# The second weighing of a block moved two places up in TensorE's order of a step

## The chip, the core and the metric

The kernel runs on one core of a Trainium2 chip. The metric is the device time of one execution in microseconds (us); of several executions the median is given. The engines are TensorE (PE; its weight loads are listed apart as PEld), VectorE (DVE), ScalarE (ACT), GpSimd (POOL) and SyncE (SP, which issues the DMAs). Each engine works through its own list of instructions in order; semaphores tie the lists together.

## What is computed

The input is x of 4 sequences of 512 tokens with 128 channels. A layer norm and an RWKV time mixing come first, then a layer norm and six layers of local attention and a gated feed-forward block, all in float32. Nearly all the time goes to the six layers; the part that this case touches is the attention:

```python
qkv = x @ Wqkv                      # 128 -> 3 * 1024, 16 heads of 64
q = l2norm(q) * qs; k = l2norm(k) * ksc
q = q * cos * scale + rotate_half(q) * sin * scale
k = k * cos * inv + rotate_half(k) * sin * inv
sim = einsum('bhwie,bhwje->bhwij', bq, bk2) * QK_SCALE   # windows of 32, each with the one before
attn = softmax(where(mask, -big, sim), -1)
out = einsum('bhwij,bhwje->bhwie', attn, bv2)
x = out @ Wo + x
```

After each attention comes `a * gelu(gate) @ W2 + b2` on a layer-normed, token-shifted x.

## The kernel before

**Blocks and steps.** An item is one sequence in one layer: 6 x 4 = 24 items. An item has 4 blocks of 128 tokens, so there are 96 blocks. The main loop (function `transformer`) runs over steps, one new block for each, software-pipelined: in step s TensorE projects block s, turns and scores q and k of block s-2, and finishes block s-3. `t = step % 4` is the place of the step in its item. The feed-forward work of an item is spread over the steps t = 3 (`centre`, `variance`), t = 0 (`widen_rstd`, `expand` 0 and 1) and t = 1 (`expand` 2, `contract`) that follow.

**What sets the order.** Every engine has a list written out by hand, one loop body for each engine. There is no scheduler. TensorE's step is, in this order: `project` V0, `project` Q0, `turn_qk(step - 2, 0)`, at t = 1 `expand` 2, at t = 3 `centre`, `project` Q1, at t = 0 `widen_rstd`, `weigh(step - 3, 1)`, `turn_o(step - 3, 0)`, `score(step - 2)`, `turn_o(step - 3, 1)`, `project` K0 and K1, `turn_qk(step - 1, 3)`, `merge_heads`, at t = 1 `contract`, `turn_probs` twice, the rest of the feed-forward, `project` V1, `turn_qk(step - 1, 2)`, `weigh(step - 2, 0)`, `turn_qk(step - 1, 1)`, at t = 0 `expand` 1.

**The calls by their lines.** `project` is three matmuls of 128x512 (L1202 to L1204). `turn_qk` is four transposes of a rotated and normed part of q or k (L1212); ACT copies the result to `q_t` or `k_t` (L1074). `score` is two mask matmuls (L1236) and 64 small matmuls q by k (L1246). `weigh` is 32 small matmuls of probabilities by v (L1284) into `wide`. Each small matmul stands in the trace as two weight loads and two matmuls, so `weigh` is 64 loads and 64 matmuls and `score` is 128 and 128. `turn_o` is four transposes of the weighed values (L1299), `merge_heads` the output projection (L1313), `widen_rstd` four transposes (L1341) that wait for the root of the norms, DVE's L922. `expand` is L1357 and L1358, `centre` L1324.

**The waits around `weigh(g, 1)`.** It waits only for `o_normed[0]` of its block: DVE must have read the first half of `wide` (L946, L949) before the second weighing overwrites it. Its own result goes to DVE's second L946 and L949. DVE's step is: nine small operations of the root (L914 to L922), `rotate` 0 (L879, L885), L946 and L949 for half 1, `rotate` 1, `maximum` (L928) twice, `shift` (L936) and sums of squares (L895), `rotate` 2 and 3, and at its end L946 and L949 for half 0 of the next block. ACT copies both halves of q (L1074) ahead of `square` 0 (L1064) and the first copy of o (L1095). `turn_o(g, 0)` waits for `o_normed[0]` and for the copy of the first half of q, whose bank it writes; `score` waits for the copies of all four parts of q and k, and for several reads of its two banks.

Of the kernel before, what the change touches and what calls it, by code (L numbers as in the profile page):

```python
# [82 lines left out]
def need(eng, sem, value, most=None):  # L83

    value = value if most is None else min(value, most)
    if value > 0:
        eng.wait_ge(sem, value)
# [531 lines left out]
def transformer(nc, bank, wide, weights, w_qkv, w_o, w_1, w_2, ident, center, mean_col, x_state, vecs, qk_rows,  # L619
# [12 lines left out]
    with ExitStack() as ctx:  # L632
# [59 lines left out]
        def live(g):  # L692
            return 0 <= g < BLOCKS
# [487 lines left out]
        def _(pe):  # L1181
# [24 lines left out]
            def turn_qk(g, c, before, value):  # L1206
                if not live(g):
                    return
                pe.wait_ge(normed[c], g + 1)
                need(pe, before, value)  # L1210
                for j in range(4):
                    mm = pe.transpose(bank[2 + c % 2][:, j * P:(j + 1) * P],  # L1212
                                      qk[:, g % 2, c, j * P:(j + 1) * P], ident[:])
                mm.then_inc(qk_turned[c], 1)
# [120 lines left out]
            def widen_rstd(m):  # L1335
                if not real(m):
                    return
                g = NBLK * (m + 1) + NBLK - 1
                pe.wait_ge(rooted, root_count(g))
                for j in range(NBLK):  # L1340
                    mm = pe.transpose(bank[4][:, j * P:(j + 1) * P],  # L1341
                                      rnorm[:, g % 2, NORMS + j:NORMS + j + 1].to_broadcast([P, P]), ident[:])
                mm.then_inc(rstd_wide, 1)
# [36 lines left out]
            for step in range(STEPS):  # L1380
                item, t = divmod(step, NBLK)
                project(step, V0)
                project(step, Q0)
                turn_qk(step - 2, 0, qk_taken[2], step - 1)
                if t == 1:
                    expand(item - 2, 2)
# [2 lines left out]
                project(step, Q1)  # L1389
                if t == 0:  # L1390
                    widen_rstd(item - 2)
                weigh(step - 3, 1)
                turn_o(step - 3, 0)
                score(step - 2, step)
                turn_o(step - 3, 1)
# [46 lines left out]
```

## Time and profile before

| | before |
|---|---|
| median of 3 runs | 1769.03 us (1767.48 to 1780.83) |
| the profiled execution: whole time | 1768.05 us |
| the profiled execution: span | 1766.3 us |
| mean granted TensorE clock | 0.97 of full |
| PE busy | 1612.7 us (91%) |
| DVE busy | 1445.9 us (82%) |
| ACT busy | 1106.9 us (63%) |
| POOL busy | 998.8 us (57%) |

The span is the time from the first to the last instruction of the profiled execution. Busy time is the time in which an engine has an instruction running. The chain is followed back from the last instruction, at each step to what released it; "issue" in it is time in which the engine waited for nothing that the profile shows.

### The profile page before, as it was taken

How to read it: one execution, taken by the hardware profiler on the slowest of the kernel's cores; microseconds unless marked ns; L12 is line 12 of the kernel's file. 1: busy time of each engine (PE TensorE's matmuls, PEld its weight loads, DVE VectorE, ACT ScalarE, POOL GpSimd, SP SyncE). 2: the span in 40 equal slices, each digit the busy share in tenths (PEclk: the TensorE clock that was granted, in tenths of full speed). 3: DMA queues.
4: the chain of work that ended last, by engine and by line, in shares of the span. 5: the costliest groups of instructions: out<-in, count | busy, mean ns of one | idle time of the engine just before them, and what ended most of it. 6: DMA issues, size and time to landing. Idle time of an engine off the chain costs nothing.

```text
span 1766.3 us, 75410 instructions
## 1 busy us (share of the span) xinstructions
PE 1612.7 (91%) x31917; PEld 1243.7 (70%) x32013; DVE 1445.9 (82%) x3189; ACT 1106.9 (63%) x1990; POOL 998.8 (57%) x956
## 2 busy tenths in 40 slices
PE   5369998999899999999999999999999999999985
PEld 2137776777777777777778777777777777777763
DVE  8769887888788888888888888888888888878861
ACT  5236666667566666666766766666766666766652
POOL 2246655665556566556576567476467476465530
PEclk8579999999999999999999999999999999999997
DMA  3011101111111111201111111111111111011010
GB/s 103 26 52 37 51 24 48 45 42 36 51 36 39 48 35 39 60 24 51 48 36 40 39 45 51 44 40 39 36 47 52 40 43 39 28 50 51 24 45 13
DMA packets 40597, 74.95 MB, mean 42 GB/s; under 512 B 8992, under 2 KB 22088, under 8 KB 40264
## 3 DMA queue, kind: packets, MB, share of 16 engines
q1 hardware_dynamic: 40264, 70.11, 13.6%
q8 instruction: 257, 4.21, 1.0%
q14 instruction: 76, 0.62, 0.1%
HBM read 20.08 MB, written 2.10 MB: 13 GB/s over the span
## 4 chain that ended last, share of the span: by engine, by line
PE 82%; issue 5%; DVE 4%; POOL 2%; ACT 1%; DVEq 0%; POOLq 0%; ACTq 0%
PE bank L1212 9%; PE bank L1313 9%; PE wide L1284 8%; PE bank L1246 8%; PE bank L1202 7%; PE bank L1204 7%; PE bank L1203 7%; PE bank L1299 6%; PE bank L1264 4%; PE bank L1357 4%; PE bank L1358 4%; PE bank L1368 4%; PE bank L1236 2%; PE bank L1324 1%; PE bank L1332 1%
## 5 line engine op out<-in xcount | busy, mean ns | idle before, releaser
L795 POOL TENSOR_TENSOR qk<-qk,qk_sin 128x512 f32<-128x512 f32 x384 | 492.2, 1282 | 215.4 <-DVE qk_sin L885 215.4
L803 POOL TENSOR_TENSOR qk<-qk,rnorm 128x512 f32<-128x512 f32 x384 | 401.8, 1047 | 352.9 <-DVE rnorm L922 352.9
L1064 ACT ACTIVATE squares<-bank 128x512 f32<-128x512 f32 x384 | 229.1, 597 | 159.1 <-DVE qk_sin L885 157.3
L1202 PE MATMUL bank<-w_hi,xs_hi 128*128 128x512 f32 x576 | 290.4, 504 | 12.9 <-ACT squares L1064 6.9
L895 DVE TENSOR_REDUCE norm<-squares 128x8 f32<-128x512 f32 x384 | 258.3, 678 | 31.1 <-ACT squares L1064 28.9
L879 DVE TENSOR_TENSOR qk<-bank,tables 128x512 f32<-128x512 f32 x384 | 261.5, 681 | 6.4 <-PE bank L1204 5.4
L885 DVE TENSOR_TENSOR qk_sin<-bank,tables 128x512 f32<-128x512 f32 x384 | 261.0, 680 | 0.0
L1212 PE MATMUL bank<-ident,qk 128*128 128x128 f32 x1536 | 237.2, 278 | 2.6 <-POOL qk L803 1.8
L1204 PE MATMUL bank<-w_hi,xs_lo 128*128 128x512 f32 x576 | 230.3, 400 | 0.0
L1203 PE MATMUL bank<-w_lo,xs_hi 128*128 128x512 f32 x576 | 228.1, 396 | 0.0
L1212 PEld LDWEIGHTS bank<-ident,qk 128*128 128x128 f32 x1536 | 185.5, 142 | 51.2 <-issue 3.2
L1246 PEld LDWEIGHTS bank<-k_t,q_t 64*32 64x32 f32 x12288 | 131.3, 105 | 96.7 <-issue 96.2
L928 DVE TENSOR_REDUCE row_max<-bank 128x8 f32<-128x512 f32 x192 | 123.6, 686 | 91.9 <-PE bank L1246 91.7
L1246 PE MATMUL bank<-k_t,q_t 64*32 64x64 f32 x12288 | 154.7, 226 | 47.8 <-issue 47.4
L1313 PE MATMUL bank<-o_t,w_o_s 128*128 128x128 f32 x1536 | 193.3, 280 | 2.9 <-DVE probs L936 1.8
L1095 ACT COPY o_t<-bank 128x512 f32<-128x512 f32 x192 | 112.2, 584 | 123.2 <-PE bank L1299 123.0
L1313 PEld LDWEIGHTS bank<-o_t,w_o_s 128*128 128x128 f32 x1536 | 181.1, 194 | 5.4 <-issue 4.1
L1284 PEld LDWEIGHTS wide<-v,p_t 64*32 64x32 f32 x12288 | 134.4, 106 | 50.1 <-issue 47.9
L1284 PE MATMUL wide<-v,p_t 64*32 64x65 f32 x12288 | 166.1, 225 | 2.8 <-DVE o L949 1.1
L1080 ACT ACTIVATE probs<-probs 128x512 f32<-128x512 f32 x192 | 121.0, 631 | 63.6 <-DVE probs L936 57.5
L1202 PEld LDWEIGHTS bank<-w_hi,xs_hi 128*128 128x128 f32 x576 | 110.2, 191 | 52.8 <-issue 27.8
L1056 ACT COPY v<-bank 128x512 f32<-128x512 f32 x192 | 113.8, 592 | 49.4 <-PE bank L1204 48.9
(161 smaller groups left out, 2563.2 us busy)
## 6 DMA issues: line engine op xcount, KB each, us to landing
v<-v SPq DMA_DIRECT2D x96, 390.0 KB, 3.5
v<-v SPq DMA_DIRECT2D x72, 130.0 KB, 3.6
w_raw<-in_L_ffn_Wqkv SPq DMA_DIRECT2D x36, 256.0 KB, 3.7
w_o_s<-in_L_ffn_Wo SPq DMA_DIRECT2D x6, 512.0 KB, 5.0
w_s<-in_L_ffn_W SPq DMA_DIRECT2D x6, 341.0 KB, 5.0
mix_x_nat<-in_L_attn_x SPq DMA_DIRECT2D x4, 256.0 KB, 3.4
x_res_scratch<-mix_x_res SPq DMA_DIRECT2D x4, 256.0 KB, 2.8
w_raw<-x_res_scratch SPq DMA_DIRECT2D x4, 256.0 KB, 4.5
```

What stands on the lines that cost most here:

```text
L795: pool.tensor_tensor(qk[:, g % 2, c, :], qk[:, g % 2, c, :], qk_sin[:, c, :], ALU.add).then_inc(added[c], 1)
L803: pool.tensor_tensor(view, view, rnorm[:, g % 2, c * HPC:(c + 1) * HPC].unsqueeze(2) .to_broadcast([P, HPC, DH]), ALU.mult).then_inc(norme ...
L879: dve.tensor_tensor(qk[:, g % 2, c, :].rearrange("p (h d) -> p h d", d=DH), src[:].rearrange("p (h d) -> p h d", d=DH), table(kind).unsque ...
L885: dve.tensor_tensor(qk_sin[:, c, :].rearrange("p (h a d) -> p h a d", a=2, d=DH // 2), src[:].rearrange("p (h a d) -> p h a d", a=2, d=DH ...
L895: dve.tensor_reduce(norm2[:, c * HPC:(c + 1) * HPC], squares[:, c % 2, :].rearrange("p (h d) -> p h d", d=DH), AX.X, ALU.add).then_inc(sum ...
L1202: pe.matmul(bank_of(c)[:], l_hi, w_hi[:, n, :], start=True, stop=False)
L1203: pe.matmul(bank_of(c)[:], l_hi, w_lo[:, n, :], start=False, stop=False)
L1204: pe.matmul(bank_of(c)[:], l_lo, w_hi[:, n, :], start=False, stop=True).then_inc(projected[c], 1)
L1212: mm = pe.transpose(bank[2 + c % 2][:, j * P:(j + 1) * P], qk[:, g % 2, c, j * P:(j + 1) * P], ident[:])
L1246: mm = pe.matmul(bank[4 + r][WINDOW * h:WINDOW * (h + 1), col:col + 2 * WINDOW], q_t[row, pair, WINDOW * w:WINDOW * (w + 1)], k_t[row, pai ...
L1284: mm = pe.matmul(wide[WINDOW * h:WINDOW * (h + 1), w, quad * (DH + 1):(quad + 1) * (DH + 1)], p_t[row, r, 2 * s + m, WINDOW * h:WINDOW * ( ...
L1313: mm = pe.matmul(bank[4][:, 0:P], w_o_s[:, layer % 2, p, :], o_t[:, g % 2, p, :], start=(p == 0), stop=(p == PAIRS - 1))
```

## The change

One call in TensorE's list is written at another place. The instructions are the same, in every engine, and the lists of the other four engines are unchanged.

```diff
                 project(step, V0)
                 project(step, Q0)
+                weigh(step - 3, 1)
                 turn_qk(step - 2, 0, qk_taken[2], step - 1)
                 if t == 1:
                     expand(item - 2, 2)
...
                 project(step, Q1)
                 if t == 0:
                     widen_rstd(item - 2)
-                weigh(step - 3, 1)
                 turn_o(step - 3, 0)
                 score(step - 2, step)
                 turn_o(step - 3, 1)
```

TensorE's list in a step t = 2 of the kernel before, from the transposes of q's first half (bank2) to the scores; what an instruction waits for stands in brackets.

```order
L1212 MATMUL bank2<-ident,qk 128x128 [waits qk_taken2,normed0]
L1212 MATMUL bank2<-ident,qk 128x128 x3
L1202 MATMUL bank0<-w_hi,xs_hi 128x512 [waits v_taken0]
L1203 MATMUL bank0<-w_lo,xs_hi 128x512
L1204 MATMUL bank0<-w_hi,xs_lo 128x512
L1284 MATMUL wide<-v,p_t 32x65 [waits o_normed0]
L1284 MATMUL wide<-v,p_t 32x65 x31
L1299 MATMUL bank2<-ident,o 128x128 [waits qk_taken0,o_normed0]
L1299 MATMUL bank2<-ident,o 128x128 x3
L1236 MATMUL bank4<-mask_bf,ident_bf 128x512 [waits x1_done,shifted0,qk_taken3,shifted1,qk_taken2,x2_done,qk_taken1,qk_taken0]
```

The same place in the changed kernel.

```order
L1284 MATMUL wide<-v,p_t 32x65 [waits o_normed0]
L1284 MATMUL wide<-v,p_t 32x65 x31
L1212 MATMUL bank2<-ident,qk 128x128 [waits qk_taken2,normed0]
L1212 MATMUL bank2<-ident,qk 128x128 x3
L1202 MATMUL bank0<-w_hi,xs_hi 128x512 [waits v_taken0]
L1203 MATMUL bank0<-w_lo,xs_hi 128x512
L1204 MATMUL bank0<-w_hi,xs_lo 128x512
L1299 MATMUL bank2<-ident,o 128x128 [waits qk_taken0,o_normed0]
L1299 MATMUL bank2<-ident,o 128x128 x3
L1236 MATMUL bank4<-mask_bf,ident_bf 128x512 [waits x1_done,shifted0,qk_taken3,shifted1,qk_taken2,x2_done,qk_taken1,qk_taken0]
```

The weighing (L1284) has passed the transposes of q and the projection of q's second half, which now stand directly ahead of `turn_o` (L1299) and the scores. Nothing was added to a wait.

TensorE's list in a step t = 0 of the kernel before, around `widen_rstd` (L1341).

```order
L1204 MATMUL bank0<-w_hi,xs_lo 128x512
L1341 MATMUL bank4<-ident,rnorm 128x128 [waits rooted]
L1341 MATMUL bank4<-ident,rnorm 128x128 x3
L1284 MATMUL wide<-v,p_t 32x65 [waits o_normed0]
L1284 MATMUL wide<-v,p_t 32x65 x31
L1299 MATMUL bank2<-ident,o 128x128 [waits qk_taken0,o_normed0]
```

The same place in the changed kernel.

```order
L1204 MATMUL bank0<-w_hi,xs_lo 128x512
L1341 MATMUL bank4<-ident,rnorm 128x128 [waits rooted]
L1341 MATMUL bank4<-ident,rnorm 128x128 x3
L1299 MATMUL bank2<-ident,o 128x128 [waits qk_taken0,o_normed0]
```

The weighing that stood behind `widen_rstd` now stands ahead of it, with one projection and four transposes between.

## Rows read from the trace of the kernel before

**Rows 1.** The page: the span, and each engine's busy time.

```profile
span 1766.3 us, 75410 instructions
PE 1612.7 (91%) x31917; PEld 1243.7 (70%) x32013; DVE 1445.9 (82%) x3189; ACT 1106.9 (63%) x1990; POOL 998.8 (57%) x956
```

**Rows 2.** The page: the chain that ended last, share of the span by engine.

```profile
PE 82%; issue 5%; DVE 4%; POOL 2%; ACT 1%; DVEq 0%; POOLq 0%; ACTq 0%
```

**Rows 3.** Waits: engine, line <- releaser: us in total, times, longest us.

```profile
PEld bank L1246 <- issue: 96.2, 143, 3.2
...
DVE row_max L928 <- PE bank L1246: 91.7, 92, 3.9
...
DVE row_sum L946 <- PE wide L1284: 32.1, 71, 2.2
...
PEld bank L1341 <- DVE rnorm L922: 16.5, 24, 2.2
...
PE bank L1236 <- issue: 5.8, 24, 0.3
```

**Rows 4.** The page, DMA queues: packets, MB, share of 16 engines.

```profile
q8 instruction: 257, 4.21, 1.0%
```

**Rows 5.** Timeline, PEld: start us, us, line, count [idle before]; first and last late break.

```profile
189.92 0.15 PEld L1246 LDWEIGHTS bank<-k_t,q_t 64*32 64x32 f32 x8 [1.28 <-issue]
...
1653.85 0.29 PEld L1246 LDWEIGHTS bank<-k_t,q_t 64*32 64x32 f32 x30 [1.10 <-issue]
```

**Rows 6.** The same view: first and last early break.

```profile
219.65 0.57 PEld L1246 LDWEIGHTS bank<-k_t,q_t 64*32 64x32 f32 x49 [0.68 <-issue]
...
1534.82 0.70 PEld L1246 LDWEIGHTS bank<-k_t,q_t 64*32 64x32 f32 x64 [0.19 <-issue]
```

**Rows 7.** Timeline, PE, a step t = 2 with a late break.

```profile
799.08 0.86 PE L1284 MATMUL wide<-v,p_t 64*32 64x65 f32 x64
799.87 0.66 PE L1299 MATMUL bank<-ident,o 128*128 128x128 f32 x4
800.58 0.38 PE L1236 MATMUL bank<-mask_bf,ident_bf 128*128 128x512 bf16 x1
800.89 1.35 PE L1246 MATMUL bank<-k_t,q_t 64*32 64x64 f32 x113
803.50 0.34 PE L1246 MATMUL bank<-k_t,q_t 64*32 64x64 f32 x15 [1.26 <-issue]
```

**Rows 8.** DMA queues in the stretch 801.0 to 801.2 us.

```profile
q8 instruction: 1, 0.02, 33.9%
```

**Rows 9.** Timeline, PEld, a step t = 0: a wait for the root, an early break.

```profile
830.26 0.41 PEld L1341 LDWEIGHTS bank<-ident,rnorm 128*128 128x128 f32 x4 [1.37 <-DVE rnorm L922]
830.84 0.70 PEld L1284 LDWEIGHTS wide<-v,p_t 64*32 64x32 f32 x64 [0.17 <-issue]
...
832.83 0.81 PEld L1246 LDWEIGHTS bank<-k_t,q_t 64*32 64x32 f32 x73 [0.42 <-issue]
834.12 0.62 PEld L1246 LDWEIGHTS bank<-k_t,q_t 64*32 64x32 f32 x55 [0.49 <-issue]
```

**Rows 10.** DMA queues in the stretch 831.4 to 831.5 us.

```profile
q8 instruction: 1, 0.02, 91.7%
```

**Rows 11.** Timeline, PE, a step t = 2 without a break.

```profile
866.48 0.60 PE L1212 MATMUL bank<-ident,qk 128*128 128x128 f32 x4
...
867.71 0.86 PE L1284 MATMUL wide<-v,p_t 64*32 64x65 f32 x64
868.50 0.66 PE L1299 MATMUL bank<-ident,o 128*128 128x128 f32 x4
869.21 0.38 PE L1236 MATMUL bank<-mask_bf,ident_bf 128*128 128x512 bf16 x1
```

**Rows 12.** Timeline, ACT, the same step: the two copies of q.

```profile
867.12 1.07 ACT L1074 COPY q_t<-bank 128x512 f32<-128x512 f32 x2 [0.47 <-PE bank L1212]
```

**Rows 13.** Timeline: DVE's first half of o and q's transposes, step t = 3.

```profile
811.74 0.69 DVE L949 TENSOR_TENSOR o<-wide,row_sum 128x512 f32<-128x512 f32 x1
...
812.92 0.60 PE L1212 MATMUL bank<-ident,qk 128*128 128x128 f32 x4
```

## The prediction

> **What bounds the kernel now.** I read the page first: PE is busy for 1612.7 of 1766.3 us, DVE for 1445.9 [rows 1], and the chain that ended last is 82% PE and 5% issue, with only 4% DVE [rows 2]. So TensorE's own list sets the pace, and a call that only changes its place can bring time only where TensorE stands still. The waits say where that is [rows 3]. Weight loads of L1246, the scores, stood idle for 96.2 us in 143 pieces with nothing named but issue. Of these, 0.42 us a step is the regular wait ahead of the first score after the masks [rows 9], 96 x 0.42 = 40.3; the other 55.9 us are breaks inside the scores. L1341 waited 16.5 us in 24 pieces for DVE's root, and L1236 5.8 us in 24. DVE waited for the scores (91.7 us) and for the weighing (32.1 us), so in these steps it follows TensorE.
>
> **What the breaks are.** I count 50 of 0.1 us or more in the timelines. They come in two kinds. In 30, the last 4 to 31 of the score's 128 loads stand behind the break ("late"; the first and the last in [rows 5]); these make about 44 us, counted from start to start. In 20, from 46 to 69 loads do ("early"; the first and the last that the timeline shows apart in [rows 6]), about 15 us. Counting loads, matmuls and wait instructions of TensorE's list, the breaks stand 256 instructions apart or a multiple of that. TensorE has 31917 matmuls and 32013 loads [rows 1] and some 1,850 wait instructions, 257 x 256 in all, and the instruction queue moved 257 packets of 4.21 MB, 16 KB each [rows 4]. So a break is TensorE waiting for a packet with its next 256 instructions. In a late break at 802.2 to 803.5 us [rows 7] the packet started between 801.0 and 801.2 [rows 8], some 2.4 us before the scores went on. In an early one [rows 9] it started between 831.4 and 831.5 [rows 10], 2.7 us before 834.12. The packet is asked for only shortly after the block before it is entered, 256 instructions earlier. In the early case that point is about 33 instructions into the weighing that starts at 830.84, at 831.0; the packet starts 0.45 us later. In the late case it is in the weighing's last dozen instructions, at 799.6, and the packet starts 1.4 us later. Weighing and scores together hold 384 loads and matmuls in 2.4 us of work [rows 7], so 256 instructions are gone before the packet, which needs about 2.9 us or more, is there.
>
> **What the change does to them.** Between the weighing and the scores it puts the four transposes and one projection. By [rows 11] these take 867.71 - 866.48 = 1.23 us, at t = 3 0.9 us more (`centre` passes too), at t = 1 1.7 (`expand`) and at t = 0 0.6 (`widen_rstd`). The number of instructions in a step and up to the scores stays, so the block ends fall on the same scores.
>
> - *Early breaks.* Their packet is asked for inside the weighing, as now; it comes 1.2 to 2.1 us earlier against the scores. All but four of the 20 were shorter than 1.2 us. Gain: about 12 of 15 us.
> - *Late breaks.* Here the request falls behind the weighing's end, where TensorE's sequencer has to pass the waits for `turn_o` and the scores (the list shows ten) before it asks. It can run ahead of the array there. How far is not shown, so I bound it. Below: no gain. Above: the whole of 1.2 to 2.9 us for each, some 38 of 44 us. The waits include the copies of q, which now end later. At t = 2 they end just ahead of the scores, so I take nothing for these 8 breaks. At t = 0, 1 and 3 the copies end some 0.4 to 0.6 us earlier against the scores than the waits are passed now; 22 breaks x 0.55 = 12 us.
> - *New breaks.* `weigh(step - 2, 0)`, four transposes, two projections and `weigh(step - 3, 1)` now follow one another, some 290 instructions in 0.8 + 0.5 + 1.4 + 0.3 + 0.7 = 3.7 us. The packet is there 0.45 + 2.4 = 2.9 us after the boundary at best, in the longer breaks 1.5 later. For 34 of the 256 places of a boundary, 13 of 96 steps, that may break the weighing; between 0 and 13 x 0.7 = 9 us, and I take 2.5, since most packets are in time.
>
> **The other terms.**
>
> - *The root at t = 0.* The 0.79 us of the weighing (831.63 - 830.84, to the next call) now run while L1341 waits. Of its 24 waits, 17 are of 0.3 us, 5 of 1.37 [rows 9] and two in the last steps of 2.1. One weighing covers the small ones whole and 0.8 of the others: 17 x 0.3 + 5 x 0.8 + 0.8, about 9.5 us of the 16.5 [rows 3]. DVE's root stands ahead of everything that the change touches on DVE.
> - *Masks at t = 0.* The 5.8 us ahead of L1236 [rows 3] arise where the wait instructions follow directly on the weighing's 128; with a projection and slow transposes ahead they are passed in time. 5 us.
> - *The copies of q at t = 2.* The transposes start 0.79 + 0.1 us later. Now ACT copies from 867.12 to 868.19 and the masks start at 869.21 [rows 11, 12]. After the change the copies end at about 869.1, and `turn_o`, which needs the first copy, could have started at 868.5 and may at about 868.65. The cost is between 0 and 0.4 us a step; I take 0.2, nearest to the two sums: 24 x 0.2 = 5 us lost. At t = 0, 1 and 3 a call more lies between, 0.6 us at least, and it costs nothing.
> - *The weighing's own wait.* It needs the first half of o. At t = 3, where it is tightest, L949 ends at 812.43 and the weighing would start at 812.9 or so [rows 13]. Hidden by 0.4 us; if DVE came later by more than that, all that it is late would be PE's.
> - *DVE.* It gets the second half earlier and loses its 32.1 us of waits there [rows 3], but then waits for the scores instead, since their place did not move. Worth nothing by itself. It has room to follow a faster TensorE: 320 us not busy [rows 1].
> - *PE's work.* The same instructions; each change of kind (projection to transposes, to weighing, and back) occurs as often as before. 0.
>
> **Sum.** 12 + 12 - 2.5 + 9.5 + 5 - 5 = 31 us. The profiled execution took 1768.05 us as a whole, 1.75 more than its span and 0.98 under the median. 1768 - 31 = 1737; I take 1738.
>
> **Rule and row.** The breaks show the fetch of instructions on the path: a packet starts 1.4 us after its block was due to be asked for and the scores stand for 1.26 us [rows 7, 8]. The Trainium skill, Runtime: NRT & Kernel Launch, section Instruction fetch mechanics, says that TensorE holds 2048 instructions and that crossing a 16 KiB boundary is "mostly hidden". By that rule the breaks would not be fetches, would not care what stands ahead of the scores, and the sum would be 9.5 + 5 - 5, some 10 us. The same skill, Advanced Engine Details and Errata, section ISA Cache, gives only two lines of 256 instructions, and the row agrees with that one: no packet starts before the block ahead of it is about to be entered.
>
> **Rivals.**
>
> - *The breaks stay (0.24).* They may hang on the scores themselves, or the late ones may not profit and as many early ones arise anew. For: half of the delay of a late packet lies in waits that don't move away. Against: in the steps t = 1, where `expand` precedes the weighing, the boundary falls as in the early kind and yet no break stands. Time: 1768 - 10 = 1758, with half of the early gain 1752.
> - *The change does next to nothing, or less (0.06).* The copies of q cost 0.4 us at t = 2 and 0.2 at the others, 24 x 0.4 + 72 x 0.2 = 24 us, against 9.5 + 5 and a third of the breaks' gain. Time: 1770.
> - *Slower: the weighing waits for DVE (0.08).* Moved up, it comes 1.2 us and more sooner to its wait for the first half of o, and that is hidden by 0.4 us only at t = 3 [rows 13]. If the faster scores leave DVE behind, TensorE stands ahead of the weighing instead. For: DVE is busy for 82% [rows 1]. Against: it now waits for the scores 92 times in 96 steps [rows 3], so it isn't behind. It decides from 31 / 96 = 0.32 us a step, that is with DVE 0.75 us later than now at t = 3; at 0.6 us a step it costs 58 us, 27 more than all gains: 1795.
> - *The forecast (0.62).* 1720 to 1750 us. Its lower end has the late breaks gain 30 instead of 12.
>
> **The numbers.** The kernel's measurements agree within 1% or so, which is about what they can tell from no change: 1751 and 1787 are the bounds. Faster by more than 1%: the forecast and a little of the first rival, 0.64. Within 1%: the rest of it, the second and a part of the third, 0.30. Slower: 0.06, most of the third. The range runs from 1718 (all terms and most of the late gain) to 1764, which takes in the first rival and leaves out about 0.05 below and 0.13 above.
>
> **What would show it.** In the profile after: L1341's weight loads wait some 7 us instead of 16.5. L1236's issue wait is near 0. The issue waits of L1246's loads fall from 96 to about 75 us; early breaks are gone, late ones are left mostly at t = 2. DVE's wait for L1284 is near 0, that for L1246 falls by less than the breaks do. A wait of L1299 or L1236 for ACT's q_t appears at t = 2, under 0.3 us each. I would be wrong if L1246's issue wait stays at 96 (the first rival), if L1284 waits for DVE's o (the third), or if breaks of over a few us in all appear in L1284.

## The result: 1.5% slower

| | before | changed |
|---|---|---|
| median | 1772.18 us (4 runs, 1767.48 to 1780.83) | 1797.95 us (4 runs, 1791.35 to 1814.6) |
| profiled execution, span | 1766.3 us | 1799.5 us |
| ratio | | 1.0148, 95% interval 1.0099 to 1.0196 |

The forecast was 1738 us, faster. The kernel became slower by about 26 us. The median before is now that of four executions, where the table above the change had three.

The page of the changed kernel, with the lines that answer to [rows 1, 2, 4] (here and below "..." stands for lines left out): the span, the engines' busy time, the chain by engine, and the instruction queue.

```profile
span 1799.5 us, 75410 instructions
...
PE 1620.2 (90%) x31917; PEld 1242.4 (69%) x32013; DVE 1449.2 (81%) x3189; ACT 1101.2 (61%) x1990; POOL 997.2 (55%) x956
...
q8 instruction: 257, 4.21, 1.0%
...
PE 78%; issue 8%; DVE 4%; ACT 2%; POOL 2%; DVEq 0%; ACTq 0%; POOLq 0%
```

TensorE's work is the same, and its share of the chain fell from 82% to 78%; "issue" rose from 5% to 8%. So TensorE stands still longer. Its waits and those of DVE and ACT in the changed kernel, to be read beside [rows 3]:

```profile
ACT q_t L1074 <- PE bank L1212: 132.3, 96, 2.5
...
PEld bank L1246 <- issue: 96.6, 132, 2.2
DVE row_max L928 <- PE bank L1246: 91.8, 82, 3.3
...
DVE qk L879 <- PE bank L1212: 35.7, 67, 1.1
PEld bank L1236 <- issue: 34.6, 49, 1.2
...
PE bank L1236 <- DVE xc_xn L974: 23.3, 23, 1.2
...
PEld bank L1341 <- DVE rnorm L922: 4.7, 7, 2.1
...
PE bank L1236 <- ACT xc_xn L1113: 10.4, 23, 0.5
```

Four things are seen. L1341's wait fell from 16.5 to 4.7 us; I had forecast some 7. The idle time of the scores' loads stayed (96.2, now 96.6), where I had forecast 75. The masks (L1236) have two waits that did not exist: 23.3 us for DVE's L974, in 23 steps t = 0, and 10.4 us for ACT's L1113, in 23 steps t = 3. And DVE's `rotate` (L879) waits 35.7 us for q's transposes.

The waits of L1236 as a matmul need a caution. A step has two mask matmuls, 192 in all, but the trace of the kernel before has 96 of them; that is the whole difference between its 31917 matmuls and 32013 weight loads [rows 1]. The trace of `m2_only`, an experiment below whose steps t = 0 have the same list as before, has all 192. Matmuls of L1236, count, busy time and idle time, before and in `m2_only`:

```profile
L1236 PE MATMUL bank<-mask_bf,ident_bf 128*128 128x512 bf16 x96 | 36.6, 381 | 9.6 <-issue 5.8
L1236 PE MATMUL bank<-mask_bf,ident_bf 128*128 128x512 bf16 x192 | 57.0, 378 | 1.1 <-issue 0.5
```

The first mask's record is missing before, and where the engine has nothing else running, at t = 0, its 0.21 us count as idle time ahead of the second. So the 5.8 us of issue wait before the change were no idle time. The traces of the changed kernel, `all_turn_first`, `m0_turn_first`, `m1_only` and `pad30` lack the same record. Where the masks wait, that adds some 4.9 us in 23 steps: the 23.3 us stand for some 18.4, and the 10.4 for some 5.5. The weight loads are complete in all of them, and the tables below go by these.

For a sum I took, from the starts of TensorE's weight loads in the steps 6 to 93 (22 of each t), the time from the last load of Q0's projection to the masks, and the breaks inside the scores; a whole step is counted from Q0 to Q0:

| mean of a step, us | t = 0 | t = 1 | t = 2 | t = 3 | all 88 steps |
|---|---|---|---|---|---|
| Q0 to masks, before | 3.90 | 4.58 | 2.88 | 3.72 | 331.9 |
| Q0 to masks, changed | 4.40 | 4.68 | 3.32 | 4.25 | 366.4 |
| breaks in scores, before | 0.62 | 0.52 | 0.76 | 0.82 | 59.8 |
| breaks in scores, changed | 0.57 | 0.43 | 0.87 | 0.68 | 56.3 |
| whole steps, before | 18.57 | 18.18 | 14.39 | 16.21 | 1481.7 |
| whole steps, changed | 19.09 | 18.18 | 14.92 | 16.34 | 1507.9 |

The way to the masks grew by 34.5 us, the breaks shrank by 3.5 and the short piece between masks and scores by 4.3 (53.2 to 48.9). That leaves 26.7 us, and the 88 steps together took 26.2 more. The medians differ by 25.8. The spans of the two profiled executions differ by 33.2; the other 7 us lie ahead of step 6 and behind step 93, half and half, and the table says nothing of them.

A step t = 0 of the changed kernel, TensorE's timeline (start us, us, line, count, idle before):

```profile
774.98 0.91 PE L1284 MATMUL wide<-v,p_t 64*32 64x65 f32 x64
775.82 0.66 PE L1212 MATMUL bank<-ident,qk 128*128 128x128 f32 x4
...
777.01 0.60 PE L1341 MATMUL bank<-ident,rnorm 128*128 128x128 f32 x4
777.45 0.60 PE L1299 MATMUL bank<-ident,o 128*128 128x128 f32 x4
779.12 0.38 PE L1236 MATMUL bank<-mask_bf,ident_bf 128*128 128x512 bf16 x1 [1.07 <-DVE xc_xn L974]
```

and DVE's timeline there:

```profile
775.79 0.20 DVE L922 SCALAR_TENSOR_TENSOR rnorm<-root_w,rnorm 128x36 f32<-128x36 f32 x1
776.61 0.69 DVE L879 TENSOR_TENSOR qk<-bank,tables 128x512 f32<-128x512 f32 x1 [0.63 <-PE bank L1212]
777.22 0.68 DVE L885 TENSOR_TENSOR qk_sin<-bank,tables 128x512 f32<-128x512 f32 x1
777.82 0.74 DVE L974 SCALAR_TENSOR_TENSOR xc_xn<-xc_xn,vecs,bank 128x512 f32<-128x512 f32 x1
```

The root is ready at 775.99, and TensorE no longer waits for it. But L879 of `rotate` 0 overwrites the buffer that q's transposes of the block two before read, so it waits for these, which now end at 776.48. Everything behind it in DVE's list comes 0.6 us later, L974 too. L974 reads the bank that the first mask overwrites, and the masks wait for it until about 778.9 (779.12 is the second). L974 also waits for the transposes of `widen_rstd` (L1341), whose result it reads; what that does is seen in `m0_turn_first` below.

A step t = 3 of the changed kernel: TensorE, then ACT.

```profile
829.07 0.66 PE L1212 MATMUL bank<-ident,qk 128*128 128x128 f32 x4
829.57 1.02 PE L1324 MATMUL bank<-xs,center 128*128 128x512 f32 x2
...
832.18 0.38 PE L1236 MATMUL bank<-mask_bf,ident_bf 128*128 128x512 bf16 x1 [0.46 <-ACT xc_xn L1113]
```

```profile
829.77 1.07 ACT L1074 COPY q_t<-bank 128x512 f32<-128x512 f32 x2 [0.70 <-PE bank L1212]
830.73 0.62 ACT L1112 ACTIVATE xsq_gated<-bank 128x512 f32<-128x512 f32 x1
831.22 0.60 ACT L1113 COPY xc_xn<-bank 128x512 f32<-128x512 f32 x1
```

ACT stood idle for 0.70 us for the transposes, copied q, and only then read the result of `centre`, whose bank the second mask overwrites. But `centre` (L1324) is late too: it ends at 830.59, 0.14 us before L1112 starts. So two delays end at nearly the same time here, and this timeline can't tell which of them costs. ACT's wait for L1212 ahead of its q copies is 132.3 us in all in the changed kernel, against 37.8 before.

### The profile page after: what moved, and what is told of

It reads as the page before. It is cut to its first block, busy times and chain, and to the rows that moved or that the text cites. A ratio compares the mean times of both kernels' runs of the same rounds, so it can differ in the third digit from the quotient of the medians.

```text
span 1799.5 us, 75410 instructions
## 1 busy us (share of the span) xinstructions
PE 1620.2 (90%) x31917; PEld 1242.4 (69%) x32013; DVE 1449.2 (81%) x3189; ACT 1101.2 (61%) x1990; POOL 997.2 (55%) x956
## 4 chain that ended last, share of the span: by engine, by line
PE 78%; issue 8%; DVE 4%; ACT 2%; POOL 2%; DVEq 0%; ACTq 0%; POOLq 0%
PE bank L1212 10%; PE bank L1313 10%; PE wide L1284 8%; PE bank L1246 8%; PE bank L1202 7%; PE bank L1204 6%; PE bank L1203 6%; PE bank L1299 4%; PE bank L1264 4%; PE bank L1357 4%; PE bank L1358 3%; PE bank L1368 3%; PE bank L1236 2%; PE bank L1332 1%; DVE xc_xn L974 1%
## 5 line engine op out<-in xcount | busy, mean ns | idle before, releaser
L803 POOL TENSOR_TENSOR qk<-qk,rnorm 128x512 f32<-128x512 f32 x384 | 400.9, 1044 | 356.5 <-DVE rnorm L922 356.5
L879 DVE TENSOR_TENSOR qk<-bank,tables 128x512 f32<-128x512 f32 x384 | 262.6, 684 | 44.4 <-PE bank L1212 35.7
L1212 PE MATMUL bank<-ident,qk 128*128 128x128 f32 x1536 | 242.7, 281 | 2.0 <-POOL qk L803 1.2
L1212 PEld LDWEIGHTS bank<-ident,qk 128*128 128x128 f32 x1536 | 177.7, 141 | 46.9 <-issue 2.6
L1246 PEld LDWEIGHTS bank<-k_t,q_t 64*32 64x32 f32 x12288 | 129.9, 105 | 96.8 <-issue 96.6
L1074 ACT COPY q_t<-bank 128x512 f32<-128x512 f32 x192 | 105.1, 587 | 132.3 <-PE bank L1212 132.3
L1284 PEld LDWEIGHTS wide<-v,p_t 64*32 64x32 f32 x12288 | 134.7, 105 | 58.2 <-issue 54.8
L1284 PE MATMUL wide<-v,p_t 64*32 64x65 f32 x12288 | 168.3, 225 | 5.3 <-issue 3.0
```

Source lines behind the costliest of these rows:

```text
L803: pool.tensor_tensor(view, view, rnorm[:, g % 2, c * HPC:(c + 1) * HPC].unsqueeze(2) .to_broadcast([P, HPC, DH]), ALU.mult).then_inc(norme ...
L879: dve.tensor_tensor(qk[:, g % 2, c, :].rearrange("p (h d) -> p h d", d=DH), src[:].rearrange("p (h d) -> p h d", d=DH), table(kind).unsque ...
L1212: mm = pe.transpose(bank[2 + c % 2][:, j * P:(j + 1) * P], qk[:, g % 2, c, j * P:(j + 1) * P], ident[:])
L1246: mm = pe.matmul(bank[4 + r][WINDOW * h:WINDOW * (h + 1), col:col + 2 * WINDOW], q_t[row, pair, WINDOW * w:WINDOW * (w + 1)], k_t[row, pai ...
L1284: mm = pe.matmul(wide[WINDOW * h:WINDOW * (h + 1), w, quad * (DH + 1):(quad + 1) * (DH + 1)], p_t[row, r, 2 * s + m, WINDOW * h:WINDOW * ( ...
```

## The experiments

All kernels are edits of TensorE's list of the kernel before, unless said otherwise. A ratio is to the kernel before, timed beside it, with its 95% interval; the differences in us that follow are worked out from it, where no median is named. "Breaks" is the sum of the pauses of over 0.1 us inside the scores of the whole profiled execution, from the start of a load to the start of the next: 60.6 us before, 59.9 in the changed kernel. Each kernel has one profile. In the steps t = 2 and 3, whose list is that of the kernel before in `m0_only`, `m1_only` and `m0_turn_first` too, the breaks were 34.7 us before and 40.9, 41.1 and 41.3 there, so I read a difference of up to 6 us between two profiles as nothing.

**One t at a time.** `m2_only`, `m0_only`, `m3_only` and `m1_only` have this edit with another number each:

```diff
                 project(step, Q0)
+                if t == 2:
+                    weigh(step - 3, 1)
                 turn_qk(step - 2, 0, qk_taken[2], step - 1)
...
-                weigh(step - 3, 1)
+                if t != 2:
+                    weigh(step - 3, 1)
```

`m2_only`, as expected before it ran:

> The weighing moves up only in the steps t = 2. Theory A (the cost is the new waits ahead of the masks: here the copies of q, L1074): from the end of Q0's projection to the masks the step takes 3.2 us instead of 2.86, about 8 to 10 us in all, the breaks in the scores of t = 2 don't shrink (17 us before, 19 in the changed kernel), time 10 us above before. Theory B (the cost is the code packets, breaks in the scores, and the masks' waits hide behind them): the way to the masks costs less than 3 us in all and the breaks of t = 2 grow by 5 us or more. Theory C (my prediction's sum for t = 2: 5 us lost to the copies, 4 won from early breaks): 1 us.

Measured: 1.0059 (1.0040 to 1.0077), 10 us slower. Q0 to masks at t = 2 is 3.27 us, 0.39 more than before, 8.6 us in all. The breaks at t = 2 are 21 us where they were 17.

`m0_only`, as expected before it ran:

> The weighing moves up only in the steps t = 0, ahead of the transposes that wait for the root (L1341). Theory A (the scores at t = 0 wait for DVE's L974, which reads the widened root from the masks' bank, and the weighing stood between them): L1341 waits 10 us less, the masks L1236 stand 23 us for L974, the way from Q0 to the masks grows by 0.5 us a step, 11 us in all, time +10 to +12. Theory B (breaks): L1246 breaks at t = 0 grow. Theory C (my prediction): 9.5 and 5 us won, time -14.

Measured: 1.0101 (1.0075 to 1.0127), 18 us slower. The way to the masks at t = 0 grew by 0.50 us a step, 11 us. The waits of `m0_only`:

```profile
PEld bank L1246 <- issue: 104.7, 140, 2.9
...
PE bank L1236 <- DVE xc_xn L974: 18.4, 23, 1.0
...
DVE qk L879 <- PE bank L1212: 10.2, 18, 0.7
```

The scores' issue time grew too (104.7 against 96.2), with 6 us of that at t = 2 and 3, which the edit doesn't touch. So the remaining 7 us of time are not explained.

`m3_only`, as expected before it ran:

> The weighing moves up only in the steps t = 3, ahead of centre. Theory A (centre comes 0.8 us later, and the masks wait for ACT's copies L1112 and L1113 of its result, since the second mask writes the same bank): L1236 waits 10 us in 23 pieces for L1113, the way from Q0 to the masks grows by 0.5 us a step, 12 us in all; breaks at t = 3 shrink by 3 us; time +8 to +10. Theory C (my prediction): nothing at the masks, 5 to 9 us won from breaks.

Measured: 1.0066 (1.0039 to 1.0093), 12 us slower. Q0 to masks at t = 3 is 4.28 us, 0.56 more. L1236 waits 5.5 us for L1113. I had expected 10 from the changed kernel's 10.4, but that number holds the missing mask records; without them it is 5.5 there too. The breaks at t = 3 did not shrink (23 us).

`m1_only`, as expected before it ran:

> The weighing moves up only in the steps t = 1, ahead of expand 2. The changed kernel's way from Q0 to the masks was 0.1 us longer there and its breaks at t = 1 2 us shorter. Theory A: +2 us on the way, no gain from the breaks: 0 to +3 us against before. Together with m0, m2 and m3 (+18, +10, +12 us) the parts give more than the whole (+26), if breaks are what the parts share.

Measured: 1.0004 (0.9979 to 1.0030), no change. 0.10 us more on the way at t = 1 and 7.2 us of breaks there instead of 11.5. The four parts add up to 40 us, the whole change costs 26; the intervals of the parts and of the whole, taken together, allow for some 12 of the 14 between.

**The transposes out of the way.** If it is their delay that costs, putting them ahead of Q0 takes the cost away and leaves the weighing where the change put it. `m2_turn_first` does it at t = 2, `m0_turn_first` at t = 0:

```diff
                 project(step, V0)
+                if t == 2:
+                    turn_qk(step - 2, 0, qk_taken[2], step - 1)
                 project(step, Q0)
+                if t == 2:
+                    weigh(step - 3, 1)
...
```

`m2_turn_first`, as expected before it ran:

> Only at t = 2: the weighing moves up as in m2_only, but q's transposes go ahead of Q0's projection, so that the copies of q end 1.5 us earlier than there. Theory A: the way from Q0 to the masks is no longer than before (the four transposes now stand ahead of it, so 0.4 us shorter as measured from Q0, 2.4 us). Since TensorE's waits ahead of the scores are met early, its next block of code is asked for earlier, and the late breaks of t = 2 fall from 1.4-1.8 us each to under 0.5: time 8 to 14 us below before. If the breaks don't depend on these waits but on the scores alone, they stay at 17 to 20 us at t = 2 and the time is that of before.

Measured: 0.9979 (0.9959 to 0.9999), 4 us faster than before, where 8 to 14 had been expected. From `m2_only` to this is 14 us. The way from Q0 to the masks is 2.48 us with the 0.44 us of the transposes no longer in it, against 2.88 before: nothing lost. The late breaks of t = 2 are 1.15 us each, against 1.43 before and 2.0 in `m2_only`; I had expected under 0.5. In `m2_turn_first` the packet of a late break at t = 2 still starts only about when the masks run, 1.1 us after the last wait instruction was passed. So the waits of `turn_o` and the scores seem to be a part of the packets' delay, not all of it.

`m0_turn_first`, as expected before it ran:

> Only at t = 0: the weighing moves up as in m0_only, but q's transposes go ahead of Q0's projection. Theory A (in m0_only DVE's rotate 0, L879, waits for the late transposes because it overwrites what they read, so L974, which the scores at t = 0 wait for, comes late): DVE's wait for L1212 is 0, L974 comes as early as before, L1236's wait for L974 falls from 18 us to under 8, and the way from Q0 to the masks is at least 0.5 us a step shorter than in m0_only: time 10 to 14 us below m0_only (1792), some 1 to 6 us above before. If the masks wait for L974 just because the weighing no longer stands between, they go on waiting for over 15 us and the time is m0_only's.

Measured: 1.0028 (1.0006 to 1.0051), 1782 us, 10 us below `m0_only` and 5 above before. Its waits:

```profile
PE bank L1236 <- DVE xc_xn L974: 20.6, 23, 1.2
...
DVE xc_xn L974 <- PE bank L1341: 9.4, 19, 1.2
...
DVE qk L879 <- PE bank L1212: 1.4, 1, 1.4
```

DVE's wait for L1212 is all but gone and the time fell as forecast, but the masks go on waiting for L974, where I had expected under 8: 20.6 us, which without the missing records is 15.7, against 18.4 in `m0_only`. The second line says why. L974 now waits for TensorE's own L1341, 9.4 us in 19 steps (2.0 us in 2 steps before). With the weighing ahead of it, `widen_rstd` starts 0.73 us later than before, L974 0.41 us later, and between `widen_rstd` and the masks only `turn_o` is left. So the late transposes are not what holds the masks back at t = 0; the place of the weighing ahead of `widen_rstd` is, which was the second of the two expectations. Counted from V0's projection, so that the moved transposes don't matter, the masks come after 4.59 us before, 5.10 in `m0_only` and 5.00 here. What the early transposes win at t = 0 is in the breaks: 7.4 us there instead of 12.8.

In the kernel before, the first mask starts 2.1 us after the root is ready and 0.26 us after L974 has ended; `widen_rstd`, the weighing and `turn_o` filled just that time. Moved ahead of `widen_rstd`, the weighing takes away a wait of 0.3 us and opens one of 0.7.

`all_turn_first`, as expected before it ran:

> In all steps q's transposes go ahead of Q0's projection, and the weighing goes up behind centre and expand, ahead of Q1: V0, transposes, Q0, expand or centre, weighing, Q1. Theory A: no wait of DVE for L1212, none of the masks for q's copies or for L1113; the masks at t = 0 wait for L974 as in m0_turn_first. Time between 8 us below before and 4 above, some 25 to 30 below the changed kernel. Rival (it is the weighing's own place that costs, through the code packets): the time stays 15 us or more above before, with breaks grown by 10 us.

```diff
                 project(step, V0)
-                project(step, Q0)
                 turn_qk(step - 2, 0, qk_taken[2], step - 1)
+                project(step, Q0)
                 if t == 1:
                     expand(item - 2, 2)
                 if t == 3:
                     centre(item - 1)
+                weigh(step - 3, 1)
                 project(step, Q1)
                 if t == 0:
                     widen_rstd(item - 2)
-                weigh(step - 3, 1)
```

Measured: 0.9948 (0.9917 to 0.9978), 1764 us, with breaks of 48.5 us. That is 9 us below before and 34 below the changed kernel, somewhat more than expected; the rival fails.

`turn_first_only`, as expected before it ran:

> q's transposes ahead of Q0's projection in all steps, the weighing left where it was before. If the half per cent that all_turn_first won comes from the weighing's move, this is at 1.0 of before (0.997 to 1.003), with breaks of 55 to 65 us in the scores. If the earlier transposes win it, this is at 0.995 like all_turn_first.

This is `all_turn_first` with the weighing left at its old place. Measured: 0.9990 (0.9969 to 1.0011), breaks 64.7 us. So the gain is the weighing's own, though the two ratios differ by only 0.4%, just more than their intervals allow for. It lies in the breaks, 16 us fewer, of which the longer way to the masks at t = 0 takes back 9.

`keep0_turn_first`, as expected before it ran:

> all_turn_first, but at t = 0 the weighing stays behind widen_rstd. If the chain root, rotate 0, L974, masks bounds t = 0 (the masks can't start before DVE has done L974), the weighing's place at t = 0 matters little: L1236's wait for L974 (20.7 us) falls to about 0, the way from V0 to the masks at t = 0 is 0.3 to 0.5 us shorter, time 5 to 10 us below all_turn_first's. If the place at t = 0 is worth what my prediction said, it is 10 us above it.

Where its list differs from that of `all_turn_first`:

```diff
+                if t != 0:
+                    weigh(step - 3, 1)
                 project(step, Q1)
                 if t == 0:
                     widen_rstd(item - 2)
+                    weigh(step - 3, 1)
```

Measured: 0.9913 (0.9884 to 0.9942), 1760 us. The wait of L1236 for L974 is gone, L1341 waits 16.7 us again, and the median is 5 us below that of `all_turn_first`, which the intervals of the two can't tell from nothing. The way from V0 to the masks at t = 0 is 0.41 us shorter. Together with `m0_turn_first`, slower than before by 0.06% at least, this says that at t = 0 the weighing is better off behind `widen_rstd`.

**Which of the two delays costs at t = 3.**

`m3_centre_first`, as expected before it ran:

> Only at t = 3: V0, Q0, centre, weighing, transposes, Q1. Here centre is earlier than before and q's transposes are 1.6 us later. If m3_only's cost comes from the late transposes (ACT copies q ahead of centre's result in its list, so everything behind is late), the masks wait as long or longer for L1113, DVE waits for L1212, and the time is 12 us or more above before. If it comes from the late centre, the masks wait for nothing and the time is within 4 us of before.

```diff
                 project(step, Q0)
+                if t == 3:
+                    centre(item - 1)
+                    weigh(step - 3, 1)
                 turn_qk(step - 2, 0, qk_taken[2], step - 1)
...
-                if t == 3:
-                    centre(item - 1)
...
-                weigh(step - 3, 1)
+                if t != 3:
+                    weigh(step - 3, 1)
```

Measured: 1.0123 (1.0078 to 1.0167), 22 us slower, though `centre` comes earlier than before. The waits:

```profile
DVE qk L879 <- PE bank L1212: 31.4, 24, 1.7
...
PE bank L1236 <- ACT xc_xn L1113: 19.3, 23, 0.8
```

The masks wait 19.3 us for the copy of a result that was there early: ACT's list has the copies of q ahead of it. Q0 to masks at t = 3 takes 5.28 us, 1.56 more than before. So late transposes alone can hold the masks back at t = 3. Here they are 2.0 us later than before; in the changed kernel it is 1.0.

`after_turn_first`, as expected before it ran:

> The changed kernel with one further edit: q's transposes ahead of Q0's projection. Weighing, centre, expand and widen_rstd stand as in the changed kernel. If the late transposes are its whole loss but for t = 0: 1764 to 1770, close to all_turn_first (0.995 of before). If the late centre costs by itself: the masks at t = 3 wait 5 to 10 us for L1113 and the time is 5 to 10 us above all_turn_first.

This is the changed kernel with one more edit:

```diff
                 project(step, V0)
+                turn_qk(step - 2, 0, qk_taken[2], step - 1)
                 project(step, Q0)
                 weigh(step - 3, 1)
-                turn_qk(step - 2, 0, qk_taken[2], step - 1)
```

Measured: 0.9980 (0.9956 to 1.0004), 1773 us, where the changed kernel is at 1.0148. The place of the four transposes is worth 1.7%, more than the change's whole loss. Where these 1.7% lie is a further question. From the starts of the weight loads of the steps 6 to 93 again, but counted from the last load of V0's projection, so that the moved transposes don't matter:

| mean of a step, us | t = 0 | t = 1 | t = 2 | t = 3 | all 88 steps | breaks | whole steps |
|---|---|---|---|---|---|---|---|
| V0 to masks, before | 4.59 | 5.28 | 3.57 | 4.42 | 393.0 | 59.8 | 1481.7 |
| V0 to masks, changed | 5.10 | 5.38 | 4.01 | 4.95 | 427.6 | 56.3 | 1507.9 |
| V0 to masks, `after_turn_first` | 5.02 | 5.39 | 3.61 | 4.82 | 414.6 | 38.6 | 1474.3 |
| V0 to masks, `all_turn_first` | 5.01 | 5.33 | 3.61 | 4.47 | 405.1 | 46.2 | 1479.2 |

Of the 34 us that `after_turn_first` wins on the changed kernel, 13 are on the way to the masks, 9 of them at t = 2, and 18 are in the breaks. At t = 0 and t = 3 the way stays 0.43 and 0.41 us longer than before, though the transposes are early. At t = 0 that is the late `widen_rstd`, as in `m0_turn_first`. At t = 3 it is the late `centre`. ACT there, in `after_turn_first`:

```profile
ACT xsq_gated L1112 <- PE bank L1324: 21.8, 24, 2.2
```

In `all_turn_first`, with `centre` ahead of the weighing, that wait is 2.2 us, 1 time, and the way is the old one but for 0.05 us. L1113 ends 0.86 us later than before in `after_turn_first` and 0.99 later in the changed kernel. So in the changed kernel either delay alone, that of `centre` or that of the transposes, was nearly enough for what was lost at t = 3, and taking one away won little. I had expected the masks to wait 5 to 10 us for L1113 if the late `centre` costs. That wait doesn't show, only the longer way does. What it costs in time is not shown: `after_turn_first` is 0.3% above `all_turn_first`, less than their intervals allow for.

**Whether the breaks are ends of code blocks.**

`pad30`, as expected before it ran:

> The kernel before with 15 small extra matmuls (30 instructions with their weight loads, under 2 us) ahead of the main loop, which shifts every later instruction by 30. If the breaks in the scores stand at the ends of blocks of 256 instructions, each comes 15 loads earlier in its score: none is left with more than 113 loads ahead of it but a few at the start, the early ones (59 to 82 loads) move to 44 to 67 loads and mostly vanish, and the time falls by 10 to 20 us. If they belong to the scores themselves, or to times of transfers alone, the breaks keep their loads and the time is that of before.

```diff
+            for _ in range(15):
+                pe.matmul(bank[4][:, 0:P], ident_bf[:], ident_bf[:], start=True, stop=True)
             for step in range(STEPS):
```

Measured: 0.9909 (0.9885 to 0.9933), 1764 us: faster with work added. The first early break, which stood behind 79 loads at 219.65 us [rows 6], in `pad30` (weight loads of TensorE):

```profile
220.91 0.70 PEld L1246 LDWEIGHTS bank<-k_t,q_t 64*32 64x32 f32 x64 [0.42 <-issue]
221.93 0.70 PEld L1246 LDWEIGHTS bank<-k_t,q_t 64*32 64x32 f32 x64 [0.33 <-issue]
```

It stands behind 64 loads, 15 fewer, and so it is with all the others that are still there: the one that had most loads ahead of it, 125, now has 110. The breaks in the scores fell to 45.7 us. Some moved out of the scores: `turn_o` behind them (L1299), which had 0.3 us of issue wait on its loads before, has 4.7 us in 4 pieces. A break's place is fixed by the count of instructions from the start of the list. In the trace of `turn_first_only`, which is complete, all 52 breaks stand at the same place of a block of 256, to within one instruction.

`keep0_pad44`, as expected before it ran:

> keep0_turn_first with 44 instructions more ahead of the loop. By the ends of 256-instruction blocks every break comes 22 loads earlier than there: late ones at 75 to 103 loads instead of 97 to 125, early ones at 37 to 61. Breaks sum to 20 to 35 us; time 10 to 15 us below keep0_turn_first and 1.0 to 1.5% below before.

`keep0_turn_first` and 22 such matmuls. Measured: 0.9868 (0.9835 to 0.9901), 1751 us, 9 us below `keep0_turn_first` where 10 to 15 had been expected; breaks in the scores 38.1 us instead of 47.9, just above what I had expected, and 6.3 us in 8 pieces now stand in L1299 behind the scores.

**Whether the packets wait for data transfers.**

`v_late`, as expected before it ran:

> The kernel before, but SyncE issues the move of v of a block (v<-v, and the weight loads behind it) only once the next step's scores are done, over 10 us later, well ahead of its use. Theory D (the code packet of an early break waits behind this transfer, since it starts when the transfer ends): early breaks at t = 0, 2 and 3 vanish, the longest breaks (2 to 3 us, with weight loads) too, breaks fall from 60 us to 40 to 48; time 0.5 to 1% below before. Rival (the packet's start has nothing to do with the transfer): breaks and time as before.

```diff
                 sp.wait_ge(v_taken[1], g + 1)
+                need(sp, scored, 2 * g)
                 sp.dma_start(v[PAD:P, t, 0, :, :], v[0:P - PAD, t, 1, :, :]).then_inc(v_moved[t], 16)
```

Measured: 0.9948 (0.9928 to 0.9967), 1767 us; breaks 49.7 us instead of 60.6. The early breaks halved and none of them is over 1.2 us any more, where some were 1.8 to 3.3; they did not vanish. In the kernel before, the packets of all ten early breaks at t = 2 and t = 3 start within 0.45 us of the landing of the v move, or of the weight load that is issued with it.

The later move has a price. SyncE issues the weight loads of the next layer behind it, and they come later as well. GpSimd's L129, which splits the weights, waited 9.3 us for them before, and q's and k's transposes 2.3 us for GpSimd's L803. In `v_late` (one line further down each but L129):

```profile
POOL w_hi L129 <- DMA w_raw<-in_L_ffn_Wqkv: 25.7, 6, 9.8
...
PEld bank L1213 <- POOL qk L804: 13.4, 14, 1.6
```

The steps t = 0 took 10 us more in all than before (88 steps), which ate up a good part of what the breaks gave.

`keep0_pad44_v_late`, as expected before it ran:

> keep0_pad44 with SyncE's later move of v from v_late. If packets of code wait behind that transfer, breaks fall from 38 to about 28 us and the time is 5 to 9 us below keep0_pad44 (1751), 1.7 to 2.0% below before. If the two gains are of the same breaks, it is at 1751.

Measured: 0.9853 (0.9821 to 0.9884), 1749 us, with breaks of 21.3 us. The scores' loads there (L1247, since a line was added):

```profile
PEld bank L1247 <- issue: 59.3, 123, 1.9
```

Of these 59.3, 40 are the regular wait ahead of the first score. The breaks went down by 17 us from `keep0_pad44`, and the median by only 2, within the intervals. The profiled executions differ by 8 us in their spans (1749.9 and 1741.6). The price is the same as in `v_late`: the transposes' wait for GpSimd is 12.1 us, against 3.2 in `keep0_pad44`. So v's later move wins in the breaks here too, gives back about 9 us at t = 0, and the times can't tell what is left. This version has the lowest median, 1.5% below before.

## Why the prediction was wrong, step by step

- **The step that failed: what stands behind the passed calls was put at nothing.** In the prediction's own words, of the copies of q: "At t = 0, 1 and 3 a call more lies between, 0.6 us at least, and it costs nothing"; of the root: "DVE's root stands ahead of everything that the change touches on DVE". For the way to the masks the sum had 9.5 + 5 - 5, a gain of 9.5 us. It grew by 34.5 us. By the experiments this has three parts, in the 88 steps, and 2.1 us more at t = 1:
  - At t = 2 the late copies of q: priced at 5 us, measured 9.6. Only the size was off. With the transposes early it is gone (`m2_turn_first`).
  - At t = 0 the late `widen_rstd`: the way grew by 11.1 us. L974 needs both `rotate` 0 and L1341, the masks need L974, and neither was priced. The late transposes hold up `rotate` 0, but with them early 9.5 of the 11.1 us stay (`after_turn_first`).
  - At t = 3 the late `centre` and the late transposes: the way grew by 11.7 us. Both delay ACT's L1112 and L1113, for which the masks wait. With the transposes early 9.0 of these us stay, with `centre` early and the transposes later still the loss is larger (`m3_centre_first`).
- **"The root at t = 0", 9.5 us.** The wait of L1341 fell by 12 us [rows 3], more than forecast, and all of it and more came back at the masks as the wait for L974, some 18.4 us. The time between `widen_rstd` and the scores was in use. `m0_only` and `m0_turn_first` show it.
- **"Masks at t = 0", 5 us.** There was nothing to win. The 5.8 us [rows 3] are the missing record of the first mask's matmul, not idle time; in `m2_only`, with the same list at t = 0 and all records, L1236 has 0.5 us of issue wait.
- **"Early breaks", 12 of 15 us, "late breaks", 12 of 44.** Together with the new breaks the sum had a gain of 21.5 us here. Measured 3.5 us in the 88 steps, 0.7 in the whole execution. The early ones went from 15.1 to 8.1 us: at t = 0 all eight are gone; of the ten at t = 2 and 3 five are, and two are new. Of the four long ones among these (1.7 to 3.2 us) two stayed nearly as they were, one halved and one went. By `v_late` it is the data transfers that make them long, which an earlier request does not change. The late ones grew from 45.5 to 51.7 us, at t = 0 and t = 2 above all, where the masks and `turn_o` have new waits. That these waits hold back the packet is what `m2_only` and `m2_turn_first` speak for (2.0 and 1.15 us a break, 1.43 before). With the transposes early, the gain that I had in mind is there: breaks fall from 64.7 to 48.5 us between `turn_first_only` and `all_turn_first`, 16 us where I had summed 21.5. So the late transposes cost more by the breaks that they kept alive, some 18 us, than by the way to the masks, some 13.
- **"What the breaks are".** Right: `pad30` moved every one by its 15 loads. That 257 x 256 fitted the count of instructions so well was luck, since 96 records are missing from it; complete traces have 65874. The rule of the Trainium skill that I set against it, Runtime: NRT & Kernel Launch, section Instruction fetch mechanics, says that the cost of crossing a block is mostly hidden. By number that agrees with the trace, where 49 of the 256 crossings show as a break in the scores; but these 49, in runs of tiny matmuls, cost 60.6 us, so here it can't be left out of a sum.
- **"The weighing's own wait".** Right: L1284 waited 1.5 us for DVE in all of the changed kernel, 1.1 before.
- **"New breaks", 2.5 us.** Right in size: 8 pieces, 3.0 us of TensorE idle on issue ahead of L1284, against 1 piece of 1.0 before.
- **The rivals.** The only case that was slower by more than 1% was given a chance of 0.08, and its mechanism, the weighing waiting for DVE, did not come; the waits that came were those of DVE and ACT for TensorE, the other way round, and of the masks behind them. Nearest was the second rival (0.06), with 0.4 us at t = 2 for the copies of q, which is what was measured, and a loss at the other steps too.

## What to carry to other kernels

When a call is moved up, price what it passes, not only the call: follow each passed instruction to every engine that waits for it, for its result and for the buffer that it has read, and then down that engine's list to whatever stands behind. A wait that a moved call fills is only won if the time behind it wasn't in use already; here filling the wait for the root opened a longer one at the masks. An idle time in a profile is worth a count of the records around it before it enters a sum: here 5 us of it were a missing record. Where two delays end at the same place, each has to be taken away alone and both together. Dense runs of tiny matmuls should be checked against the 256-instruction blocks of code: a few instructions ahead of a loop shift where its stalls fall, and they were worth 0.9% here.

## What the runs showed of the hardware

- TensorE's code comes in packets of 256 instructions: 257 packets for 65874 loads, matmuls and waits (`turn_first_only`), with all 52 breaks at one place of a block. In the scores, 256 loads and matmuls take 1.4 us, and behind a break the scores go on 2.2 to 3.0 us after the packet starts (49 breaks before). 15 extra matmuls at the start made the kernel 0.9% faster (`pad30`).
- A code packet can be held up by data transfers of the same core: with the v move of 390 KB out of the way, the breaks fell from 60.6 to 49.7 us, and none of the early ones is over 1.2 us, where some were 1.8 to 3.3 (`v_late`).
- Unmet waits of TensorE go together with longer late breaks: at t = 2, 1.43 us each before, 2.0 with the copies of q late (`m2_only`), 1.15 with them early (`m2_turn_first`), 8 breaks in each. Why the packet of a late break still starts only when the masks run, with all waits met 1.1 us earlier (`m2_turn_first`), stays open; no run separates that.
- The trace of a kernel can lack the same record in every step: 6 of the 17 traces have 96 of the 192 mask matmuls, and where the masks had to wait, or nothing else ran, the 0.21 us of the missing one show as idle time.
